# Third position of odd steps: one VectorE add out of PSUM in place of a ScalarE copy and a GpSimd add

## The chip, the cores and the metric

The kernel runs on one core of a Trainium2 chip. The metric is the device time of one execution in microseconds (us); lower is better. Engines are called as in the profile: PE (TensorE), PEld (TensorE's weight load), DVE (VectorE), ACT (ScalarE), POOL (GpSimd) and SP (SyncE). A "q" behind a name (ACTq, SPq) is the engine's sequencer, which also issues DMAs.

## What is computed

The input x is 32 images of 384 channels of 64x64, all fp32. Each image's channels are group-normalised in 32 groups of 12, displaced by a whole number of pixels (one displacement for every 8 channels, 48 of them), convolved channel by channel with a 5x5 Gaussian kernel that belongs to the displacement, and added to x:

```python
off_round = jnp.round(offset)
disp = _displace(x.reshape(B, P, cpp, h, w), off_int).reshape(B, C, h, w)
sub = offset - off_round
d = field[None] + sub[:, None, None, :]
kernel = jnp.exp(-jnp.sum(d * d, axis=-1) / (2.0 * SIGMA ** 2))
kernel = kernel / jnp.sum(kernel, axis=(1, 2), keepdims=True)
out = lax.conv_general_dilated(disp, kw, ..., feature_group_count=C)

x = x + _L0_conv_ref(_gn(x), L0_conv_offset)
```

Displacement and Gaussian are separable, so each is one matrix along y and one along x, and the whole is two chains of matmuls.

## The kernel before

**Tiling.** The channels are cut into 16 superblocks of 24 channels (3 displacements, called positions, of 8 channels). For a superblock the 32 images go through in 16 steps of 2 images. A step's tile `xin[:, s]` has 128 partitions and 6 x 256 fp32 (1536 elements); there are 16 such slots, so a slot is reused one superblock later. There are 256 steps, in 128 pairs of an even and an odd step.

**A pair on PE** (`two_steps`), in program order: the y products of positions 1 and 2 of the even step (position 0 was done at the end of the pair before, in `begin_even`), with the sums of the statistics between them (`sum_stats`, line 632); the y products of the odd step (all line 640); `x_products(0)` and `x_products(1)` (line 651) of the even and of the odd step. PE's results lie in `ps`, PSUM, as `ps[:, v]` for the even (v = 0) and the odd step (v = 1), four banks each. The x products of positions 0 and 1 go to banks 0 and 1 of their half, those of position 2, the "third position", to banks 2 and 3. `x_done` counts twice in a step: after positions 0 and 1, and after position 2.

**The other engines.** All follow a program order written out by hand, and talk by semaphores.

- ACT: copies y out of PSUM (`copy_y`, line 563; for the odd step three lanes of four), issues the stores of the step two behind, normalises half of a later step (line 552), and copies the third position from PSUM to the buffer `x2` (`copy_third`, line 581). At a superblock's last step it also fills the y matrices of the next one (`fill_rows`, line 541), in three parts with the two copies between them.
- DVE: in each pair the last lane's y copy (`copy_last_lane`, line 462), `add_x` for the even and the odd step (line 469: PSUM of positions 0 and 1, 1024 elements, plus `xin`, into `xin`), six `bn_stats` of 512 elements (line 441) for the pair four ahead, and between the fifth and the sixth the reduction of the summed statistics (`sums`, line 451). Once in a superblock, at step 11, also `values` (line 428).
- POOL: for each of the two steps the other half of the normalisation (line 301); once in a pair the seven small instructions of the coefficients (lines 276 to 287, `rstd` line 285 the longest) and the two of the summands (lines 259 and 261), for which PE's `sum_stats` waits; then `add_third` for the even and the odd step (line 292: `x2` plus `xin` into `xin`, 512 elements). Behind `add_third` of step 3 comes `whole_distances` (`t_int`, line 234), behind that of step 5 `full_distances` (`t_full`, line 240), behind that of step 15 `column_matrices` (`ax`, line 248).
- SP: loads the slots, each as soon as its last store has landed.

**What ties them.** `result0_ready` counts third positions that are added, `result1_ready` the rest; a store waits for both. `x2_ready` counts copies into `x2` and starts at 1. Before PE overwrites `ps[:, 1]` (first y product of an odd step) and `ps[:, 0]` (`begin_even`) it waits for `x2_ready` and `result1_ready`.

Of the kernel before, what the change touches and what calls it, by code (L numbers as in the profile page):

```python
# [6 lines left out]
ALU = mybir.AluOpType  # L7
ACT = mybir.ActivationFunctionType
# [3 lines left out]
P = 128  # L12
# [9 lines left out]
QP = Q // POS  # L22
GROUPS = 2
QG = Q // GROUPS
ROW = R * HW
# [7 lines left out]
PAIR = 2  # L33
# [12 lines left out]
def displaced_conv(nc: bass.Bass, x: bass.AP, offset: bass.AP, out: bass.AP):  # L46
# [7 lines left out]
    with ExitStack() as ctx:  # L54
        def sb(name, shape, dt=F32):
            return ctx.enter_context(nc.sbuf_tensor(name, shape, dt))

        def sem(name):
            return ctx.enter_context(nc.semaphore(name))


        xin = sb("xin", [P, SLOTS, Q, ROW])
        norm = sb("norm", [P, 2, R, Q * HW])

        y = sb("y", [P, 2, POS, R, LANES, 32])
        x2 = sb("x2", [P, 2, QP, ROW])

        stats = sb("stats", [P, RING, PAIR, CHUNKS, 3 * GROUPS])
        summands = sb("summands", [P, PAIR, CHUNKS, 3 * GROUPS])
# [57 lines left out]
        ps = ctx.enter_context(nc.psum_tensor("ps", [P, 2, LANES, 512], F32))  # L127
# [22 lines left out]
        x_done = sem("x_done")  # L150
        x2_ready = sem("x2_ready")
        result0_ready = sem("result0_ready")
        result1_ready = sem("result1_ready")
# [16 lines left out]
        ADDS = 2  # L170
# [38 lines left out]
        def _(pool):  # L209
# [19 lines left out]
            def whole_distances(c):  # L229
                if c is 0:  # L230
                    pool.wait_ge(shifts, 1)
                else:
                    pool.wait_ge(made, c)
                pool.tensor_tensor(t_int[:], grid[:, None, :, :].to_broadcast([P, POS, KINDS, HW]),  # L234
                                   place[:, bass.ds(POS * c, POS), :].unsqueeze(3).to_broadcast([P, POS, KINDS, HW]),
                                   ALU.add).then_inc(dist_ready, 1)
# [52 lines left out]
            def add_third(t, s):  # L289
                pool.wait_ge(x2_ready, t + 1 + SPARE)  # L290
                at = xin[:, s, 4:6, :]
                pool.tensor_tensor(at, x2[:, s % 2], at, ALU.add).then_inc(result0_ready, 1)  # L292

            def normalise(t, s, pair, first=False):
                pool.wait_ge(coef_ready, pair + 1)
# [21 lines left out]
            def step(c, s, head, tail):  # L317
                t, p = STEPS * c + s, STEPS // PAIR * c + s // PAIR
                if not (tail and s + PAIR >= STEPS):
                    normalise(t + PAIR, (s + PAIR) % STEPS, STEPS // PAIR * c + (s + PAIR) // PAIR)  # L320
                if s % PAIR == 1:
                    if not (tail and s // PAIR + LEAD >= STEPS // PAIR):
                        coefficients(p + LEAD, (s // PAIR + LEAD) % 2)
                    if not (tail and s // PAIR + LEAD + 1 >= STEPS // PAIR):
                        make_summands(p + LEAD + 1, (s // PAIR + LEAD + 1) % RING)
                    else:

                        pool.engine_nop().then_inc(summands_ready, PAIR)
                    add_third(t - 1, s - 1)
                    add_third(t, s)  # L330
                if not tail:
                    if s == 3:
                        whole_distances(c + 1)
                    if s == 5:
                        full_distances(c + 1)
                    if s == STEPS - 1:
                        column_matrices(c + 1)
            run(step)

        @block.vector  # L340
        def _(dve):
# [124 lines left out]
            def add_x(t, s):  # L466
                dve.wait_ge(x_done, ADDS * t + 1)
                at = xin[:, s, 0:4, :].rearrange("p (k h) f -> p h k f", h=QP)
                nc.vector.tensor_tensor(at, ps[:, s % 2, 0:2].rearrange("p h (k f) -> p h k f", k=2), at,  # L469
                                        ALU.add).then_inc(result1_ready, 1)  # L470

            def all_statistics(s):
                for part in range(CHUNKS):
# [47 lines left out]
        def _(act):  # L521
# [55 lines left out]
            def copy_third(t, s, first=False):  # L577
                act.wait_ge(x_done, ADDS * (t + 1))
                if not first:
                    act.wait_ge(result0_ready, t - 1)  # L580
                nc.scalar.activation(x2[:, s % 2], ps[:, s % 2, 2:4, 0:ROW], ACT.Copy).then_inc(x2_ready, 1)  # L581

            def store(c, s, t):
                act.wait_ge(result0_ready, t + 1)
# [4 lines left out]
            def step(c, s, head, tail):  # L589
                t = STEPS * c + s  # L590
                copy_y(t, s % 2, head and s <= 1)
                if s >= BEHIND:
                    store(c, s - BEHIND, t - BEHIND)
                elif not head:
                    store(c - 1, s - BEHIND + STEPS, t - BEHIND)
                border = s == STEPS - 1 and not tail
                if border:
                    fill_rows(c + 1, 0)
                if s % PAIR == 1:
                    copy_third(t - 1, s - 1, head and s == 1)  # L600
                if border:
                    fill_rows(c + 1, 1)
                    copy_third(t, s)
                    fill_rows(c + 1, 2)
                if not (tail and s + PAIR >= STEPS):
                    normalise(t + PAIR, (s + PAIR) % STEPS, STEPS // PAIR * c + (s + PAIR) // PAIR, False)
                if s % PAIR == 1 and not border:
                    copy_third(t, s, head and s == 1)
                if not tail:
                    if s == 5:  # L610
                        square(c + 1, 0)
                    if s == 7:
                        square(c + 1, 1)
                    if s == 9:
                        exponential(c + 1)
            run(step)

            act.wait_ge(norm0_ready, TOTAL)
# [7 lines left out]
        def _(pe):  # L626
# [35 lines left out]
            def two_steps(one):  # L662

                two, three = pe.snap(one + 1), pe.snap(one + 2)
                pe.wait_ge(norm1_ready, one)
                pe.wait_ge(mats_ready[1], one)
                y_product(1, 0)
                pe.wait_ge(summands_ready, one)
                sum_stats(0)
                pe.wait_ge(mats_ready[2], one)  # L670
                y_product(2, 0)

                pe.wait_ge(x2_ready, one)
                pe.wait_ge(result1_ready, one)
                pe.wait_ge(norm0_ready, two)
                y_product(0, 1)
                pe.wait_ge(norm1_ready, two)
                y_product(1, 1)
                y_product(2, 1)
                pe.wait_ge(ax_ready, one)  # L680
                pe.wait_ge(sums_ready, one)
                pe.wait_ge(y_ready, one)
                pe.sem_inc(x_started, 1)
                x_products(0)
                pe.wait_ge(last_lane_ready, one)
                pe.wait_ge(y_ready, two)
                pe.sem_inc(x_started, 1)
                x_products(1)

                pe.wait_ge(x2_ready, two)  # L690
                pe.wait_ge(result1_ready, two)
                begin_even(three)
# [31 lines left out]
```

## Time and profile before

| what | value |
|---|---|
| median of 3 runs | 1200.35 us (1197.65 to 1202.0) |
| the profiled execution | 1203.69 us, of which the span from the first to the last instruction is 1201.8 us |
| granted TensorE clock, mean | 0.996 |
| busy share of the span: PE, POOL, DVE, ACT | 96%, 81%, 76%, 66% |
| DMA | 335 GB/s over the span, each queue about half of the 16 engines' time |

The time outside the span is 1.9 us. In the views, a row of a group has: line, engine, operation, output and inputs with their shapes, count, then busy us and mean ns of one, then the idle time of the engine just before them and what ended it. A row of the timeline has: start and length in us from the span's start, engine, line, operation; in square brackets the idle time before it and what ended that.

### The profile page before, as it was taken

The page shows a single profiled execution, that of the slowest core. Times are in us where ns is not written, and L with a number is a line of the kernel's source. Part 1 is how long each engine was busy: PE and PEld are TensorE (multiplying, and loading weights), DVE is VectorE, ACT ScalarE, POOL GpSimd, SP SyncE. Part 2 cuts the span into 40 slices and gives each one's busy share as a digit, 9 for nine tenths or more (in the row PEclk, how much of TensorE's full clock was granted, in tenths as well). Part 3 has the DMA queues.
Part 4 walks back from the last instruction along what each step waited for, and adds up shares of the span by engine and source line. Part 5 has one row for each costly group of instructions (what it writes and reads, how often), then busy time and mean ns, then how long its engine had stood idle before and what let it go on. Part 6 is the DMA issues. An engine that isn't in the chain of part 4 may idle for free.

```text
span 1201.8 us, 113371 instructions
## 1 busy us (share of the span) xinstructions
PE 1159.0 (96%) x50224; PEld 1129.6 (94%) x50224; DVE 913.3 (76%) x1338; ACT 792.8 (66%) x915; POOL 970.4 (81%) x1734
## 2 busy tenths in 40 slices
PE   1899999999999999999999999999999999999997
PEld 1899999999999999999999999999999999999997
DVE  7578777777877777877777877777777777877773
ACT  3477667676666676666676666666666766666654
POOL 5488878878887888878878888887888888788874
PEclk9899999999999999999999999999999999999999
DMA  6899999999999999999999999999999999999966
GB/s 211 283 337 350 347 351 349 348 353 345 351 341 348 349 344 351 344 352 346 352 344 344 353 343 347 352 345 351 341 352 347 346 350 350 343 347 345 344 205 209
DMA packets 409760, 402.92 MB, mean 335 GB/s; under 512 B 16529, under 2 KB 409745, under 8 KB 409745
## 3 DMA queue, kind: packets, MB, share of 16 engines
q1 hardware_dynamic: 204944, 201.41, 51.6%
q10 hardware_dynamic: 204800, 201.36, 48.9%
q14 instruction: 13, 0.10, 0.0%
q8 instruction: 3, 0.05, 0.0%
HBM read 201.38 MB, written 201.33 MB: 335 GB/s over the span
## 4 chain that ended last, share of the span: by engine, by line
PE 89%; POOL 3%; issue 2%; ACTq 2%; ACT 1%; POOLq 0%; DVE 0%; DVEq 0%
PE ps L640 58%; PE ps L651 29%; PE ps L632 2%; ACTq L587 2%; POOL t_full L240 1%; ACT ay L541 1%; ACT x L581 1%; POOL norm L301 0%; POOL rstd L285 0%; POOL xin L292 0%; POOL summands L259 0%; POOL summands L261 0%; DVE stats L441 0%; POOLq L54 0%; POOL spread L281 0%
## 5 line engine op out<-in xcount | busy, mean ns | idle before, releaser
L640 PE MATMUL ps<-ay,norm 32*128 32x128 f32 x24608 | 762.0, 276 | 11.8 <-ACT x L581 6.3
L640 PEld LDWEIGHTS ps<-ay,norm 32*128 32x128 f32 x24608 | 723.0, 188 | 21.6 <-issue 13.4
L563 ACT ACTIVATE y<-ps 128x1536 f32<-128x1536 f32 (+1 forms) x256 | 330.2, 1290 | 257.2 <-PE ps L640 257.1
L441 DVE BATCH_NORM_STATS2 stats<-xin 128x6 f32<-128x512 f32 x768 | 487.4, 691 | 0.0
L651 PE MATMUL ps<-ax,y 64*64 64x64 f32 x24576 | 408.9, 220 | 4.4 <-issue 4.4
L651 PEld LDWEIGHTS ps<-ax,y 64*64 64x64 f32 x24576 | 389.4, 135 | 21.7 <-issue 4.6
L469 DVE TENSOR_TENSOR xin<-ps,xin 128x1024 f32<-128x1024 f32 x256 | 313.4, 1224 | 98.4 <-PE ps L651 98.1
L301 POOL TENSOR_SCALAR norm<-xin,rstd,bias 128x768 f32<-128x768 f32 x256 | 260.5, 1020 | 127.3 <-PE ps L640 107.4
L292 POOL TENSOR_TENSOR xin<-x,xin 128x512 f32<-128x512 f32 x256 | 320.3, 1272 | 11.2 <-ACT x L581 10.9
L552 ACT ACTIVATE norm<-xin,bias,rstd 128x768 f32<-128x768 f32 x256 | 261.7, 1022 | 34.9 <-issue 34.3
L581 ACT ACTIVATE x<-ps 128x512 f32<-128x512 f32 x256 | 151.0, 590 | 85.9 <-PE ps L651 85.7
L451 DVE TENSOR_REDUCE both<-ps 128x12 f32<-128x144 f32 x128 | 39.4, 308 | 136.8 <-ACT y L563 134.4
L285 POOL TENSOR_TENSOR rstd<-var,mhalf 128x4 f32<-128x4 f32 x128 | 130.2, 1017 | 10.0
L462 DVE COPY y<-ps 128x384 f32<-128x384 f32 x128 | 71.3, 557 | 41.5 <-PE ps L640 41.5
L632 PE MATMUL ps<-summands,ones 32*128 32x36 f32 x1040 | 47.9, 246 | 20.6 <-POOL summands L261 20.5
L632 PEld LDWEIGHTS ps<-summands,ones 32*128 32x128 f32 x1040 | 44.5, 190 | 22.8 <-issue 16.1
L541 ACT ACTIVATE ay<-t_msk,same 128x256 f32<-128x256 f32 x96 | 44.7, 523 | 12.3 <-issue 10.4
L261 POOL TENSOR_TENSOR summands<-stats 128x12 f32<-128x12 f32 x128 | 27.2, 213 | 19.5 <-POOL summands L259 19.3
L281 POOL TENSOR_TENSOR spread<-inner,both 128x4 f32<-128x4 f32 x128 | 26.0, 203 | 10.7
L234 POOL TENSOR_TENSOR t_int<-grid,place 128x960 f32<-128x960 f32 x16 | 28.8, 1800 | 7.0 <-DVEq L408 7.0
L283 POOL TENSOR_TENSOR var<-spread,mean_sq 128x4 f32<-128x4 f32 x128 | 26.4, 206 | 10.0
L278 POOL TENSOR_SCALAR inner<-both 128x4 f32<-128x4 f32 x128 | 25.4, 199 | 10.8
(54 smaller groups left out, 223.3 us busy)
## 6 DMA issues: line engine op xcount, KB each, us to landing
xin<-in_x_dram SPq DMA_DIRECT2D x512, 384.0 KB, 6.8
out_dram<-xin ACTq DMA_DIRECT2D x512, 384.0 KB, 6.8
off<-in_L_conv_offset_dram SPq DMA_DIRECT2D x1, 48.0 KB, 3.6
```

What stands on the lines that cost most here:

```text
L285: pool.tensor_tensor(rstd[:, v], var[:, v], mhalf[:, :], ALU.pow).then_inc(small, 1)
L292: pool.tensor_tensor(at, x2[:, s % 2], at, ALU.add).then_inc(result0_ready, 1)
L301: pool.tensor_scalar(norm[:, s % 2, :, cols].rearrange("p r (q w) -> p q r w", w=HW), xin[:, s, QG:].rearrange("p q (r w) -> p q r w", w=H ...
L441: nc.vector.bn_stats(stats[:, s // PAIR % RING, s % PAIR, n, :], xin[:, s].rearrange("p (g q) f -> p q f g", g=GROUPS)[:, n]).then_inc(bn_ ...
L462: nc.vector.tensor_copy(y[:, 1].rearrange("p k r a m -> p a (k r) m")[:, LANES - 1], ps[:, 1, LANES - 1, 0:POS * P].rearrange("p (n m) -> ...
L469: nc.vector.tensor_tensor(at, ps[:, s % 2, 0:2].rearrange("p h (k f) -> p h k f", k=2), at, ALU.add).then_inc(result1_ready, 1)
L552: nc.scalar.activation(norm[:, s % 2, :, cols].rearrange("p r (q w) -> p q r w", w=HW), xin[:, s, 0:QG].rearrange("p q (r w) -> p q r w", ...
L563: nc.scalar.activation(y[:, v].rearrange("p k r a m -> p a (k r) m")[:, 0:lanes], ps[:, v, 0:lanes, 0:POS * P].rearrange("p a (n m) -> p a ...
L581: nc.scalar.activation(x2[:, s % 2], ps[:, s % 2, 2:4, 0:ROW], ACT.Copy).then_inc(x2_ready, 1)
L632: last = nc.tensor.matmul(ps[:, v, a, SUMS], ones[rows, :], summands[rows].rearrange("p t n s -> p (t n s)"), start=True, stop=True)
L640: last = nc.tensor.matmul(ps[:, v, a, P * k:P * (k + 1)], norm[rows, v, r, P * k:P * (k + 1)], ay[rows, k, r, :], start=(r == 0), stop=(r ...
L651: last = nc.tensor.matmul(ps[outs, v, 2 * (k // 2) + h, at:at + HW], y[rows, v, k, r].rearrange("p a m -> p (a m)")[:, outs], ax[rows, k], ...
```

## The change

The third position of odd steps no longer goes by ACT's copy to `x2` and POOL's add. DVE adds it itself: in `add_x` of an odd step it waits for the second count of `x_done` and adds `ps[:, 1, 2:4, 0:256]` (512 elements a partition) to `xin[:, s, 4:6]`, and only then counts `result1_ready`. `x2` becomes a single buffer, ACT and POOL count for two steps at once (`then_inc(..., PAIR)`), and PE's wait for `x2_ready` in the middle of the pair goes away, since `result1_ready` covers it.

```diff
-        x2 = sb("x2", [P, 2, QP, ROW])
+        x2 = sb("x2", [P, QP, ROW])
...
             def add_third(t, s):
                 pool.wait_ge(x2_ready, t + 1 + SPARE)
                 at = xin[:, s, 4:6, :]
-                pool.tensor_tensor(at, x2[:, s % 2], at, ALU.add).then_inc(result0_ready, 1)
+                pool.tensor_tensor(at, x2[:], at, ALU.add).then_inc(result0_ready, PAIR)
...
                     add_third(t - 1, s - 1)
-                    add_third(t, s)
...
             def add_x(t, s):
                 dve.wait_ge(x_done, ADDS * t + 1)
                 at = xin[:, s, 0:4, :].rearrange("p (k h) f -> p h k f", h=QP)
-                nc.vector.tensor_tensor(at, ps[:, s % 2, 0:2].rearrange("p h (k f) -> p h k f", k=2), at,
-                                        ALU.add).then_inc(result1_ready, 1)
+                added = nc.vector.tensor_tensor(at, ps[:, s % 2, 0:2].rearrange("p h (k f) -> p h k f", k=2), at,
+                                                ALU.add)
+                if s % PAIR == 1:
+
+                    dve.wait_ge(x_done, ADDS * (t + 1))
+                    at = xin[:, s, 4:6, :]
+                    added = nc.vector.tensor_tensor(at, ps[:, 1, 2:4, 0:ROW], at, ALU.add)
+                added.then_inc(result1_ready, 1)
...
-                nc.scalar.activation(x2[:, s % 2], ps[:, s % 2, 2:4, 0:ROW], ACT.Copy).then_inc(x2_ready, 1)
+                nc.scalar.activation(x2[:], ps[:, 0, 2:4, 0:ROW], ACT.Copy).then_inc(x2_ready, PAIR)
...
                 if border:
                     fill_rows(c + 1, 1)
-                    copy_third(t, s)
                     fill_rows(c + 1, 2)
...
-                if s % PAIR == 1 and not border:
-                    copy_third(t, s, head and s == 1)
...
-                pe.wait_ge(x2_ready, one)
                 pe.wait_ge(result1_ready, one)
                 pe.wait_ge(norm0_ready, two)
                 y_product(0, 1)
```

On POOL the place is the end of the pair of steps 4 and 5, where `t_full` stands behind the adds. Before:

```order
81 L261 TENSOR_TENSOR summands<-stats 128x12
82 L292 TENSOR_TENSOR xin<-x,xin 128x512 x2
83 L240 TENSOR_TENSOR t_full<-t_int,sub 128x960
84 L301 TENSOR_SCALAR norm<-xin,rstd,bias 128x3x4x64 x2
85 L276 TENSOR_TENSOR mean_sq<-both 128x4
```

The same place of the changed kernel:

```order
81 L261 TENSOR_TENSOR summands<-stats 128x12
82 L292 TENSOR_TENSOR xin<-x,xin 128x512
83 L240 TENSOR_TENSOR t_full<-t_int,sub 128x960
84 L301 TENSOR_SCALAR norm<-xin,rstd,bias 128x3x4x64 x2
85 L276 TENSOR_TENSOR mean_sq<-both 128x4
```

One add of 512 elements is left ahead of `t_full`, and everything behind it moves up by one instruction.

On DVE the place is any pair, here the first of the program, from the reduction on. Before:

```order
55 L451 TENSOR_REDUCE both<-ps 128x12 [waits stat_summed,y_ready,coef_ready]
56 L441 BN_STATS stats<-xin 128x6
57 L462 COPY y<-ps 128x12x32 [waits y_done]
58 L469 TENSOR_TENSOR xin<-ps,xin 128x2x2x256 [waits x_done] x2
59 L441 BN_STATS stats<-xin 128x6 [waits first_summands,loaded8]
60 L441 BN_STATS stats<-xin 128x6 x2
```

The same place of the changed kernel:

```order
55 L450 TENSOR_REDUCE both<-ps 128x12 [waits stat_summed,y_ready,coef_ready]
56 L440 BN_STATS stats<-xin 128x6
57 L461 COPY y<-ps 128x12x32 [waits y_done]
58 L468 TENSOR_TENSOR xin<-ps,xin 128x2x2x256 [waits x_done] x2
59 L474 TENSOR_TENSOR xin<-ps,xin 128x512 [waits x_done]
60 L440 BN_STATS stats<-xin 128x6 [waits first_summands,loaded8]
```

A third add stands between the odd step's add and the six `bn_stats`, with a wait of its own. PE's own instructions stay as they are.

## Rows read from the trace of the kernel before

**Rows 1.** The page: busy us, share of the span, instructions.

```profile
PE 1159.0 (96%) x50224; PEld 1129.6 (94%) x50224; DVE 913.3 (76%) x1338; ACT 792.8 (66%) x915; POOL 970.4 (81%) x1734
```

**Rows 2.** Timeline of PE alone, from step 2's x products on, and the last pair.

```profile
196.69 3.35 PE L651 MATMUL ps<-ax,y 64*64 64x64 f32 x192
199.98 2.09 PE L640 MATMUL ps<-ay,norm 32*128 32x128 f32 x64
...
205.79 3.03 PE L651 MATMUL ps<-ax,y 64*64 64x64 f32 x192
208.75 2.08 PE L640 MATMUL ps<-ay,norm 32*128 32x128 f32 x64
210.64 0.34 PE L632 MATMUL ps<-summands,ones 32*128 32x36 f32 x8
...
214.56 3.03 PE L651 MATMUL ps<-ax,y 64*64 64x64 f32 x192
217.53 2.07 PE L640 MATMUL ps<-ay,norm 32*128 32x128 f32 x64
219.82 0.43 PE L632 MATMUL ps<-summands,ones 32*128 32x36 f32 x8 [0.22 <-POOL summands L261]
...
1191.31 3.03 PE L651 MATMUL ps<-ax,y 64*64 64x64 f32 x192
```

**Rows 3.** Waits of PE and of its weight loads: us in total, times, longest.

```profile
PE ps L640 <- ACT x L581: 6.3, 16, 0.7
...
PEld ps L632 <- POOL summands L261: 6.5, 10, 3.3
```

**Rows 4.** Timeline, POOL, steps 5 to 7.

```profile
210.40 2.49 POOL L292 TENSOR_TENSOR xin<-x,xin 128x512 f32<-128x512 f32 x2
...
212.86 1.79 POOL L240 TENSOR_TENSOR t_full<-t_int,sub 128x960 f32<-128x960 f32 x1
...
214.65 1.95 POOL L301 TENSOR_SCALAR norm<-xin,rstd,bias 128x768 f32<-128x768 f32 x2
...
217.86 1.02 POOL L285 TENSOR_TENSOR rstd<-var,mhalf 128x4 f32<-128x4 f32 x1
...
219.56 0.21 POOL L261 TENSOR_TENSOR summands<-stats 128x12 f32<-128x12 f32 x1 [0.15 <-POOL summands L259]
```

**Rows 5.** Timeline, POOL, an odd step's normalisation that waits for PE.

```profile
197.00 0.98 POOL L301 TENSOR_SCALAR norm<-xin,rstd,bias 128x768 f32<-128x768 f32 x1 [1.21 <-PE ps L640]
```

**Rows 6.** Groups by form: the adds of POOL and of DVE.

```profile
L292 POOL TENSOR_TENSOR xin<-x,xin 128x512 f32<-128x512 f32 x256 | 320.3, 1272 | 11.2 <-ACT x L581 10.9
L469 DVE TENSOR_TENSOR xin<-ps,xin 128x1024 f32<-128x1024 f32 x256 | 313.4, 1224 | 98.4 <-PE ps L651 98.1 <-issue 0.2
```

**Rows 7.** Timeline, DVE, an ordinary pair.

```profile
213.56 0.31 DVE L451 TENSOR_REDUCE both<-ps 128x12 f32<-128x144 f32 x1 [0.89 <-ACT y L563]
...
214.76 0.56 DVE L462 COPY y<-ps 128x384 f32<-128x384 f32 x1 [0.27 <-PE ps L640]
...
217.19 1.23 DVE L469 TENSOR_TENSOR xin<-ps,xin 128x1024 f32<-128x1024 f32 x1 [0.18 <-PE ps L651]
```

**Rows 8.** Timeline, a pair in which DVE also runs `values`.

```profile
168.27 0.31 DVE L451 TENSOR_REDUCE both<-ps 128x12 f32<-128x144 f32 x1 [0.97 <-ACT y L563]
...
170.16 0.56 DVE L462 COPY y<-ps 128x384 f32<-128x384 f32 x1
```

**Rows 9.** One line's view of `rstd` (ns min/median/max).

```profile
L285 POOL TENSOR_TENSOR rstd<-var,mhalf x128: 1007/1017/1029, 19.4 to 1176.3; 128x4 f32<-128x4 f32 x128
```

**Rows 10.** Timeline, PE's first y products behind a superblock's border.

```profile
616.05 2.07 PE L640 MATMUL ps<-ay,norm 32*128 32x128 f32 x64 [0.27 <-ACT x L581]
```

**Rows 11.** Timeline, the end of the program.

```profile
1193.68 2.66 POOL L292 TENSOR_TENSOR xin<-x,xin 128x512 f32<-128x512 f32 x2 [6.10 <-ACT x L581]
1193.94 1.23 DVE L469 TENSOR_TENSOR xin<-ps,xin 128x1024 f32<-128x1024 f32 x1 [0.17 <-PE ps L651]
...
1194.98 3.15 ACTq L587 DMA_DIRECT2D out_dram<-xin  x4
```

## The prediction

> **What bounds the kernel now.** The page's busy shares come first: PE is busy for 96% of the span, no other engine over 81% [rows 1]. So time is won or lost only where PE's stream is longer than it need be, and the next view is the timeline of PE alone. The pair that begins with the x products at 205.79 ends where the next x products begin, at 214.56, that is after 8.77 us. The reader is to see its parts: 2.96 us of x products (205.79 to 208.75), 1.89 us until the sums of the statistics (208.75 to 210.64), and 3.92 us from there to the next x products [rows 2]. I take 8.77 us as PE's floor for a pair. From 205.79 to the last pair's x products at 1191.31 there are 109 pairs, so 9.04 us a pair [rows 2]: 0.27 us over the floor, about 34 us over the 126 full-speed pairs of the run.
>
> Where that excess lies decides the worth of the change. Three places:
>
> 1. *The sums wait for the summands, in the pair of steps 6 and 7.* There the y products begin at 217.53 and the sums at 219.82, after 2.29 us and not 1.89: PE stands for 0.40 us [rows 2]. The view of waits says who is late: PE's weight loads waited for POOL's summands 10 times, 6.5 us in all, 3.3 of them once [rows 3], and that one is the start of the program. So 9 of 16 superblocks lose 0.36 us, together 3.2 us.
> 2. *The superblock's border.* PE waits there for ACT's copy of the even step's third position, 6.3 us in 16 waits [rows 3], for instance 0.27 us at 616.05 [rows 10].
> 3. *Slower streams.* The rest, some 24 us, is in no wait: the same 192 x products take 3.29 us from 196.69 to 199.98 and 2.96 us from 205.79 to 208.75 [rows 2]. What slows them the views of before do not tell. Neither of the odd step's third-position instructions can overlap them, since both come after the odd step's x products.
>
> **Part by part.**
>
> *POOL loses one add a pair*, 1.272 us of mean length [rows 6], 163 us of work. POOL is not PE's bound in an ordinary pair: its odd normalisation waits for PE there (1.21 us in the pair at 196.69, where it starts 0.31 us after the x products [rows 2, 5]), and coefficients and summands follow it. An earlier end of the adds changes nothing for them, since the waiting normalisation stands in between. Only where a third long instruction is in that queue does the backlog reach the summands. At step 5 it does: the two adds start at 210.40, `t_full` at 212.86, the two normalisations run back to back from 214.65 to 216.60, and the summands end at 219.77, 0.05 us before PE's sums [rows 2, 4]. Without the second add (1.23 us of the 2.49) `t_full` runs from 211.63 to 213.42, the even normalisation to 214.40, and the odd one is again released by PE, at 214.56 + 0.31 = 214.87, so that it ends at 215.85 and not 216.60. All behind it moves up by 0.75 us, the summands to 219.02. PE would want them at 217.53 + 1.89 = 219.42. The 0.40 us are gone, with 0.4 to spare. *Term: -3.2 us.* If the seven visits too short for the view of waits have a little each, it is nearer 4.
>
> *ACT loses one copy a pair.* In ordinary pairs it comes last, ahead of a wait for PE. At the border, two of the three fills of the y matrices lie behind the even copy, for which PE waits, and nothing is taken from ahead of it. *Term: 0; the 6.3 us stay.*
>
> *PE loses one wait*, for the copy of the odd step a pair back, long done. *Term: 0.*
>
> *DVE gains one add a pair.* The trace has none of this shape. From below: half of the same add at 1024 elements, 0.61 us [rows 6]. From above: that whole add, 1.22, or what POOL takes for the same elements, 1.27 [rows 6]. Two rows of DVE reading PSUM give a line between: 384 elements in 0.56 us [rows 7], 1024 in 1.224 [rows 6], so 1.04 ns an element and, for 512, 0.69 us. I take that. The Trainium skill ("VectorE: DVE Perf Modes", the section on the TRN2 errata) charges VectorE 120 cycles ahead of a PSUM source and 58 ahead of an SBUF one, which speaks against moving work there; by it the add would be 0.66 us, an estimate, and the sum would not change. The wait for `x_done` costs nothing: the second count comes with the last x products (208.75 in one pair), and the first odd add ends later.
>
> Who pays for the 0.69 us? Behind the new add stand five `bn_stats`, then the reduction, the sixth `bn_stats`, the last-lane copy. The `bn_stats` work four pairs ahead and nobody waits for them. The reduction stood idle 0.89 us for ACT's y copy in an ordinary pair and 0.97 us in the pair with `values` [rows 7, 8]. It absorbs the add with about 0.2 us left, and the last-lane copy, which has another 0.27 us of idle time in an ordinary pair, starts as before. PE itself waits for the odd adds only before the next odd step's first y product. In the pair at 214.56 the old add ends at 218.42 [rows 7], the new one at 219.11, and that product comes behind the sums (219.82) and one y product of the even step. *Term: 0.* If the cover is gone it costs, above all in the pair with `values`: there the copy ends at 170.72, 1.45 us after the x products began, about where the odd step's half of them begins. At the upper bound of 1.27 the reduction would be 0.3 us late, 16 times: +5 us. The term lies between 0 and +5.
>
> *The end.* POOL's two last adds end at 1196.34, and DVE's last odd add would end at 1195.86 [rows 11]. But ACT has four DMAs to issue from 1194.98 on, 3.15 us in a row, so the last pair of them is hardly earlier [rows 11]. *Term: 0 to -0.1.*
>
> **Sum.** 1203.69 us for the profiled execution (span 1201.8 plus 1.9) less 3.2 gives 1200.5. The profiled execution is 3.3 us above the median of the runs, so against 1200.35 the forecast is 1197.2, 0.27% less. I take differences under 0.3%, 3.6 us, as none that a measurement of this kernel can tell; the forecast lies just inside, and a little more than my sum (4 us in place of 3.2) lies outside.
>
> **Rivals.**
>
> - *Given back in the streams.* The 24 us of slow x products depend on something that is not constant from pair to pair, and the freed pair is followed by another 0.4 us sooner. If that one runs like 196.69 (+0.33 us) in each superblock, 16 times, +5.3 us stand against -3.2: 1202.5, no change that can be told. For it: fast and slow streams stand two pairs from each other, so their state is short-lived [rows 2]. Against it: nothing links it to POOL. If two pairs more of eight go that way it is +10.6 - 3.2, 1207.7, slower. The same cause can go the other way: one pair in eight less slow gives 1192.
> - *DVE becomes the late one*, the case on the other side. The place is the last-lane copy in the pair with `values`. It decides from a price of about 0.97 us for the new add with its wait; at 1.27 it is +5, net +1.6, 1202. To be slower by over 3.6 us it would have to take 1.4 us, over every row, or be joined by the first rival.
> - *DVE's new add holds POOL up.* It runs (218.42 to 219.11 in that pair) just where POOL works on bias and summands. In an ordinary pair these are ready at 210.45 for sums at 210.64, so about 0.14 us after the hand-over are free; a POOL that stood for the whole 0.69 us would cost PE 0.55 us a pair, +66 us, 1263. Against it: an add of the same kind ran from 217.19 to 218.42 [rows 7] beside `rstd` at 217.86, which took 1.02 us [rows 4], and the longest of all 128 took 1.029 [rows 9]. The Trainium skill ("SBUF — State Buffer", Who interferes with whom) has a DVE instruction contend with GpSimd when both its inputs lie in SBUF; the new add has one in PSUM, so by that rule it does not, and the trace agrees.
> - *More is freed than I see.* If POOL and ACT, with less to do, also shorten the border (half of 6.3), it is 1194.
>
> **How the numbers follow.** The forecast as worked out, the stall gone and all else within 2 us: 0.50, at 1197.2, of which nearly half is beyond 0.3%. Given back in part or whole: 0.23, 1198 to 1203. More freed, or streams faster: 0.15, 1189 to 1194. DVE late: 0.06. Two pairs in eight slower: 0.05. POOL held up: 0.01. Faster by over 0.3%: 0.40; within: 0.46; slower: 0.14. The range leaves out the ends of these: 1190 to 1204.
>
> **What would show it.** PE's sums in the pair of steps 6 and 7 start 1.89 us after the y products in every superblock, and the waits for POOL's summands have only those of the start left. POOL busy falls by about 160 us to near 810, ACT by 75, DVE rises by about 85 to near 1000. The new add reads 0.69 us. The reduction's idle time falls from 0.9 to about 0.2 us and nothing behind it is late. The waits at the border stay near 6 us. The prediction is wrong if PE shows a wait for DVE's last-lane copy, if `rstd` or the summands get longer, or if the mean of the x products' streams moves.

## The result, and the profile after

The changed kernel took 1203.94 us in the median of 20 runs (1201.01 to 1207.43), the kernel before 1200.89 us (1197.45 to 1203.6, 20 runs). The ratio is 1.0031, with a 95% interval from 1.0023 to 1.0039: slower by about 3.7 us, where a time shorter by 3.2 us was forecast.

The page of the changed kernel begins with the busy shares, which answer to [rows 1]:

```profile
PE 1163.0 (97%) x50224; PEld 1135.4 (94%) x50224; DVE 990.0 (82%) x1466; ACT 737.4 (61%) x787; POOL 813.9 (68%) x1606
```

Its groups by line follow, with those of the x products, of POOL's adds, of the reduction and of the new add:

```profile
L653 PE MATMUL ps<-ax,y 64*64 64x64 f32 x24576 | 417.9, 221 | 3.4 <-issue 3.4
...
L292 POOL TENSOR_TENSOR xin<-x,xin 128x512 f32<-128x512 f32 x128 | 162.6, 1270 | 8.7 <-ACT x L586 8.7
...
L450 DVE TENSOR_REDUCE both<-ps 128x12 f32<-128x144 f32 x128 | 39.4, 308 | 58.5 <-ACT y L568 56.0
L474 DVE TENSOR_TENSOR xin<-ps,xin 128x512 f32<-128x512 f32 x128 | 87.1, 681 | 0.0
```

And the waits of PE and its weight loads, which answer to [rows 3]:

```profile
PE ps L642 <- ACT x L586: 6.4, 16, 0.6
...
PEld ps L634 <- POOL summands L261: 3.5, 2, 3.3
```

Nearly all that was said of the engines is there. The new add takes 0.681 us. POOL is busy for 156 us less and DVE for 77 more. ACT is busy for 55 us less, not 75: the group of its copies fell by 75 (151.0 to 76.0 us), but in the records a copy overlaps its neighbours by about 0.1 us on either side, and what overlaps counts once in the share. The reduction still waits for ACT, 56 us in place of 134, so nothing behind it is late. PE's waits for the summands are gone but for the start of the program. The border is the same. And PE is busy for 4 us longer: its x products take 417.9 us in place of 408.9, with the same 24576 instructions, while its y products and sums take 1.9 and 1.4 us less. These are the x products and the reduction in the kernel before:

```profile
L651 PE MATMUL ps<-ax,y 64*64 64x64 f32 x24576 | 408.9, 220 | 4.4 <-issue 4.4
...
L451 DVE TENSOR_REDUCE both<-ps 128x12 f32<-128x144 f32 x128 | 39.4, 308 | 136.8 <-ACT y L563 134.4 <-PE ps L632 2.4
```

PE's timeline of the changed kernel, from step 6's x products on, shows both sides. The columns are start and length:

```profile
222.12 3.28 PE L653 MATMUL ps<-ax,y 64*64 64x64 f32 x192
225.33 2.09 PE L642 MATMUL ps<-ay,norm 32*128 32x128 f32 x64
227.22 0.34 PE L634 MATMUL ps<-summands,ones 32*128 32x36 f32 x8
...
231.14 3.37 PE L653 MATMUL ps<-ax,y 64*64 64x64 f32 x192
234.44 2.09 PE L642 MATMUL ps<-ay,norm 32*128 32x128 f32 x64
```

The sums start 1.89 us after the y products (225.33 to 227.22), but the x products before them take 3.21 us, and in the next pair 3.30, where the floor is 2.96 [rows 2].

For all pairs but the first I took the same distances from the records of the trace. Two sums of them are used from here on. The **stream excess** is the time from the 97th to the last record of a pair's 192 x products (the odd step's half) over 1.36 us, which is what the fastest pairs need; the first 96 of the 192 take the same time in both kernels. The **summands' stall** is the time from the y products' start behind the x products to the next x products, over 5.82 us; the only wait of PE in that stretch is the one for the summands.

| kernel | stream excess | summands' stall | border and other waits ahead of the y products |
|---|---|---|---|
| before | 17.7 us | 4.4 us | 8.0 us |
| changed | 26.7 us | -0.1 us | 7.4 us |

The sum of the differences is +9.0 - 4.5 - 0.6 = +3.9 us, at 4.0 before rounding. From the second pair's x products to the last's the trace of the kernel before shows 1138.75 us and that of the changed one 1142.76, so these three hold the whole difference. (The start of the program, up to the second pair's x products, is 2.4 us shorter in this trace; it lies between 48.2 and 52.6 us in the 13 traces of this case.)

### The profile page after: what moved, and what is told of

The parts are those of the page before. It is cut to its first block, busy times and chain, and to the rows that moved or that the text cites. A ratio compares the mean times of both kernels' runs of the same rounds, so it can differ in the third digit from the quotient of the medians.

```text
span 1203.6 us, 113103 instructions
## 1 busy us (share of the span) xinstructions
PE 1163.0 (97%) x50224; PEld 1135.4 (94%) x50224; DVE 990.0 (82%) x1466; ACT 737.4 (61%) x787; POOL 813.9 (68%) x1606
## 4 chain that ended last, share of the span: by engine, by line
PE 92%; ACTq 2%; issue 2%; ACT 1%; DVE 0%; DVEq 0%
PE ps L642 60%; PE ps L653 30%; ACTq L592 2%; PE ps L634 2%; ACT x L586 1%; ACT ay L546 0%; DVE xin L468 0%; ACTq L182 0%; DVEq L54 0%; ACT y L568 0%; ACTq L585 0%; ACTq L544 0%; ACTq L567 0%; ACTq L554 0%
## 5 line engine op out<-in xcount | busy, mean ns | idle before, releaser
L653 PE MATMUL ps<-ax,y 64*64 64x64 f32 x24576 | 417.9, 221 | 3.4 <-issue 3.4
L653 PEld LDWEIGHTS ps<-ax,y 64*64 64x64 f32 x24576 | 398.1, 135 | 20.9 <-issue 3.5
L292 POOL TENSOR_TENSOR xin<-x,xin 128x512 f32<-128x512 f32 x128 | 162.6, 1270 | 8.7 <-ACT x L586 8.7
L586 ACT ACTIVATE x<-ps 128x512 f32<-128x512 f32 x128 | 76.0, 594 | 82.4 <-PE ps L653 81.2
L474 DVE TENSOR_TENSOR xin<-ps,xin 128x512 f32<-128x512 f32 x128 | 87.1, 681 | 0.0
```

The costliest lines, as they stand in the source:

```text
L292: pool.tensor_tensor(at, x2[:], at, ALU.add).then_inc(result0_ready, PAIR)
L474: added = nc.vector.tensor_tensor(at, ps[:, 1, 2:4, 0:ROW], at, ALU.add)
L586: nc.scalar.activation(x2[:], ps[:, 0, 2:4, 0:ROW], ACT.Copy).then_inc(x2_ready, PAIR)
L653: last = nc.tensor.matmul(ps[outs, v, 2 * (k // 2) + h, at:at + HW], y[rows, v, k, r].rearrange("p a m -> p (a m)")[:, outs], ax[rows, k], ...
```

## What is different where the streams are slow

In the second half of the x products the engines do the same work at the same moments in both kernels: the even step's add on DVE, the even copy on ACT, and but for two pairs of eight the coefficients on POOL. (The even copy starts 0.1 to 0.3 us later in the changed kernel, but it waits for x products of this very half.) Nor is it the clock: two windows of the kernel before, a slow and a fast run of x products, have 1.00 of it granted (the third column from the end):

```profile
196.69:199.98 3.29, 3.29 (x197) 3.22 (x193) 2.15 (x3) 2.66 (x4) 2.66 (x7) 1.00 1.07 367
205.79:208.75 2.96, 2.96 (x197) 2.89 (x193) 2.11 (x3) 2.35 (x4) 2.63 (x8) 1.00 1.06 357
```

Two things differ. The first is in ACT's program ahead of the odd step's y copy. `REGISTER_ALU` is an instruction of the sequencer that computes the value which a wait compares with. Before:

```
125 L560 REGISTER_ALU
126 L563 ACTIVATE y<-ps 128x3x12x32 [waits x_done,y_done]
127 L587 ISA [waits result1_ready,result0_ready]
128 L587 DMA out_dram<-xin 64x6x256
```

The changed kernel:

```
114 L565 REGISTER_ALU
115 L567 REGISTER_ALU [waits y_done]
116 L568 ACTIVATE y<-ps 128x3x12x32 [waits x_done]
117 L592 ISA [waits result1_ready,result0_ready]
```

The removed odd copy waited for `x_done` to reach 2(t+1), the very value that the next odd y copy waits for. The register with it was reused. With the copy gone the value has to be computed anew, behind the wait for `y_done`, where it delays the y copy and the store behind it. The timelines of ACT and of the loads show by how much. Before, with x products from 214.56 on:

```profile
214.69 1.13 ACT L563 ACTIVATE y<-ps 128x1152 f32<-128x1152 f32 x1
214.88 1.66 ACTq L587 DMA_DIRECT2D out_dram<-xin  x2
...
215.23 1.79 SPq L194 DMA_DIRECT2D xin<-in_x_dram  x2
```

After, with x products from 231.14 on:

```profile
231.35 1.13 ACT L568 ACTIVATE y<-ps 128x1152 f32<-128x1152 f32 x1
231.56 1.52 ACTq L592 DMA_DIRECT2D out_dram<-xin  x2
...
231.48 1.39 SPq L194 DMA_DIRECT2D xin<-in_x_dram  x2
```

The y copy starts 0.21 us into the x products and not 0.13, the store is issued at 0.42 and not 0.32. The second thing is the load: here it goes out 0.34 us in, just ahead of the store, while in the fast pair of the kernel before it came at 0.67, behind it. Counted over all pairs, odd steps' loads that go out 0.2 to 0.5 us into the x products are 82 of 126 after and 51 before. Pairs with such a load have a stream excess of 0.26 us after and 0.24 before, the others 0.12 and 0.07. I call these 0.2 to 0.5 us the slow phase of the loads. Three theories follow. Theory A: the register instruction, by moving the store, makes more pairs fall into the slow phase. Theory B: it is the missing stall that lets them drift there. Theory C: the new add on DVE does it by its traffic.

## Experiments

All ratios are to the kernel before, with 95% intervals. The stream excess and the summands' stall are those of one execution of each kernel, the profiled one. There is no E7 in the table: it was E11 with its two waits on SP in the other order, and it has no time.

| run | median us | ratio | stream excess | summands' stall |
|---|---|---|---|---|
| E1 before, store 0.15 us later | 1203.73 | 1.0026 (1.0015 to 1.0038) | 16.2 us | 5.7 us |
| E2 changed, register value given back | 1196.54 | 0.9973 (0.9960 to 0.9986) | 16.0 us | 0.2 us |
| E3 changed, odd loads behind the x products | 1191.67 | 0.9929 (0.9914 to 0.9944) | 5.1 us | 0.7 us |
| E4 before, the same delay | 1197.56 | 0.9982 (0.9970 to 0.9994) | 1.8 us | 11.2 us |
| E5 E2 and E3 together | 1191.43 | 0.9921 (0.9906 to 0.9935) | 2.6 us | 0.1 us |
| E6 changed, POOL's load as before | 1203.10 | 1.0022 (1.0011 to 1.0032) | 25.1 us | 0.0 us |
| E8 E2, odd loads held to the middle | 1186.90 | 0.9882 (0.9866 to 0.9898) | 3.0 us | 0.7 us |
| E9 before, loads held to the middle | 1195.85 | 0.9958 (0.9941 to 0.9974) | 1.6 us | 13.2 us |
| E10 changed, loads held to the middle | 1191.54 | 0.9922 (0.9906 to 0.9939) | 5.1 us | 1.0 us |
| E11 E2, loads forced to the slow phase | 1203.19 | 1.0020 (1.0003 to 1.0038) | 22.3 us | 0.3 us |
| E12 changed, nearly no loads | 1186.46 | 0.9884 (0.9865 to 0.9903) | 5.2 us | 2.2 us |

**E2, the register value alone.** The wait of the removed copy stays in its place on ACT, where nothing follows but a wait for PE:

```diff
                     normalise(t + PAIR, ...)
+                if s % PAIR == 1 and not border:
+                    act.wait_ge(x_done, ADDS * (t + 1))
```

> The changed kernel with the wait of the removed odd copy left in its place on ScalarE (the wait alone), which gives the odd step's y copy its register value again; the order of ScalarE's instructions ahead of the odd store is then that of before, and the store is issued 0.31 us after the x products begin. Theory A: the excess of the odd x products falls back to 17 to 20 us, the stall at steps 6 and 7 stays away, and the time is 1195 to 1198 (0.996 to 0.998), the forecast. Theory B and theory C: still 1203 to 1205, excess near 27.

It came as theory A said. The y copy and the store are back at 0.13 and 0.32 us into x products that begin at 219.84:

```profile
219.97 1.13 ACT L568 ACTIVATE y<-ps 128x1152 f32<-128x1152 f32 x1
220.16 1.48 ACTq L592 DMA_DIRECT2D out_dram<-xin  x2
```

and the x products need 10.5 us less than in the changed kernel:

```profile
L655 PE MATMUL ps<-ax,y 64*64 64x64 f32 x24576 | 407.4, 220 | 3.0 <-issue 3.0
```

At 0.9973 the kernel is where the forecast put the change (1197.2). DVE's add and the missing stall are both in it, with an excess of 16.0 us, so theories B and C are out as the cause of the slow streams. The edit gives back the wait and, with it, the value; the two were not tried apart. That it is the value is read from the programs and from the y copy, which starts 0.13 us into the x products with it and 0.21 without.

**E1, the same lateness put into the kernel before.**

```diff
                 if not first:
+                    if v == 1:
+                        act.wait_ge(x_done, ADDS * (t - 1) - 1)
                     act.wait_ge(x_done, ADDS * (t - 1))
```

> The kernel before with one redundant wait more ahead of the odd step's y copy on ScalarE, so that its sequencer issues the odd step's store about 0.1 us later, as in the changed kernel (0.42 us and not 0.31 us after the x products begin). Theory A (the changed kernel lost a cached register on ScalarE, its store is issued behind SyncE's load and not ahead of it, and the pairs lock into the phase in which the odd x products run slowly): the excess of the odd x products rises from 17.7 us to about 25 us, with POOL, DVE and PE's waits as before, and the time to about 1206 (1.005). Theory B (it is the missing 0.4 us stall at steps 6 and 7 that lets the pairs drift into the slow phase): no change beyond 0.2%, 1200 to 1203, excess near 18. Theory C (the new VectorE add slows PE or the DMAs): as B.

The total was slower, between theory A's 1206 and the 1200 to 1203 of the others, and not by the route that theory A gave. The extra wait cost more than 0.1 us: the store goes out 0.47 us in and not 0.32, the y copy ends at 1.39 us in place of 1.26, and the odd step's half of the x products begins 0.04 us late in each pair, 4 us in all. The summands' stall is 1.3 us larger. The streams' excess did not rise (16.2 us). So lateness of the store does not by itself bring the slow phase: only 64 of 126 loads went out at 0.2 to 0.5 us, with an excess of 0.15 us. This part of theory A fell; what E1 shows is that the y copy has no slack of 0.13 us.

The traces hold one thing more: what goes with a slow stream is less the load's moment than its distance from the store. In E1 the loads that go out 0.25 to 0.35 us in have an excess of 0.12 us, where those of the same moments have 0.27 in the kernel before and 0.25 in the changed one. One such pair of E1, with x products of 3.15 us from 211.89, a load at 0.32 and a store at 0.47:

```profile
211.89 3.21 PE L653 MATMUL ps<-ax,y 64*64 64x64 f32 x192
...
212.36 1.46 ACTq L589 DMA_DIRECT2D out_dram<-xin  x2
...
212.21 1.39 SPq L194 DMA_DIRECT2D xin<-in_x_dram  x2
```

Sorted by whether the odd load goes out within 0.15 us of the odd store, before or behind it, the pairs are these:

| kernel | store, us into the x products | pairs with a load that near | their excess | excess of the others |
|---|---|---|---|---|
| E1 | 0.47 | 43 | 0.18 us | 0.11 us |
| before | 0.32 | 47 | 0.25 us | 0.08 us |
| E2 | 0.32 | 55 | 0.21 us | 0.07 us |
| E11 | 0.32 | 71 | 0.24 us | 0.10 us |
| E6 | 0.42 | 75 | 0.26 us | 0.13 us |
| changed | 0.42 | 77 | 0.26 us | 0.15 us |

The distance was chosen with the traces at hand, and no run set it by itself.

**E6, POOL's load.** An add of 512 elements on constants into a spare buffer stands behind the even step's add, its result unused.

```diff
                     add_third(t - 1, s - 1)
+                    pool.wait_ge(spare_done, p + 1)
+                    pool.tensor_tensor(spare..., twice, twice, ALU.add).then_inc(spare_done, 1)
```

> The changed kernel in which GpSimd runs, behind the even step's add, an add of the same 512 elements on constants into a spare buffer (its result goes nowhere), so that its load is that of before. Theory B (the stall at steps 6 and 7 keeps the pairs out of the slow phase): the stall is back, about 3 us, but the excess of the odd x products falls to 18, and the time to 1199 to 1201. Theory A: the stall is back and the excess stays near 25, so 1205 to 1208.

The streams stay slow, as theory A has it, but the stall did not come back, the time is no longer than the changed kernel's, and theory B is not tested by this run: the dummy takes 1.04 us and not 1.27, and where the x products take 0.25 us longer, PE comes to the sums that much later. The slow streams hide POOL's lateness. The kernel before has it too: the stall of 0.40 us at 219.82 follows x products of 2.97 us [rows 2].

**E3 and E4, the loads moved out of the way.** SP holds the load of an odd step's slot until the x products of the pair in which it would go out are done:

```diff
                     sync.wait_ge(stored[s], 16 * B * c)
+                    if s % PAIR == 1:
+                        sync.wait_ge(x_done, ADDS * (STEPS * (c - 1) + s + 5))
                     load(c, s)
```

> The changed kernel, in which SyncE issues an odd step's load not when its slot's store has landed (about 0.3 us into the x products) but when the x products of that pair are done, about 3 us in. Theory A and theory B share that the slow odd x products come with loads issued 0.2 to 0.4 us into the x products: both then expect the excess to fall below 10 us and the time to about 1185 (0.987). If the slow stream has nothing to do with the moment of the loads (theory C): no change, 1204.

> The kernel before with the same delay of the odd steps' loads. If the phase of the loads sets the speed of the odd x products in both kernels: about 1190, and 3 to 4 us slower than the changed kernel with the same delay, which is the stall at steps 6 and 7 alone. If not: 1201.

The excess falls in both, below 10 us as expected, though the totals fell less: the waits ahead of the y products, for ACT's even copy, grew to 14.9 us in E3 and 13.6 in E4, and in E4 the summands' stall grew to 11.2 us. The views of waits have these two:

```profile
PE ps L644 <- ACT x L588: 10.4, 23, 0.7
...
PE ps L642 <- ACT x L583: 10.3, 18, 0.8
```

At the border PE waits 9.6 us in E3 and 10.4 in E4, where it was 7.2 in the changed kernel and 6.7 before. The x products end 0.2 us sooner there than with slow streams, but the copy, with a fill of the y matrices ahead of it, ends 3.4 to 3.5 us after they begin in all four. So fast streams lose some 3 us of their gain at the border. In E3 most of the rest is in two other pairs, where the issues of the odd stores end 0.1 us later than in the changed kernel, and the even copy with them. E3 is 6.7 us above the 1185 expected, E4 7.6 us above its 1190. Between the two, the stall makes -10.5 us, the streams +3.3 and the waits ahead of the y products +1.3: E3 is 5.9 us faster, by the medians too.

**E5, both edits.**

> The changed kernel with both edits: the wait left in the place of the odd copy on ScalarE, and the odd steps' loads delayed until the x products of the pair are done. Theory A (the speed of the odd x products hangs on how loads and stores meet): with the loads out of the way the 0.1 us of ScalarE's issue no longer matters, so this is the same as the delay alone, 1190 to 1193, excess near 5 us. A theory in which ScalarE's extra register instruction costs time by itself expects a further 5 to 8 us, 1184 to 1187.

E5 and E3 cannot be told apart (1191.43 and 1191.67), as theory A had it; 1184 to 1187, for a register instruction that costs 5 to 8 us by itself, did not come.

**E9, E10 and E8, the odd loads held until the even step's x products are done** (`+ 4` in place of `+ 5`). They go out 1.83 us into the x products in every pair, as here in E8:

```profile
202.57 3.03 PE L657 MATMUL ps<-ax,y 64*64 64x64 f32 x192
...
204.40 1.91 SPq L194 DMA_DIRECT2D xin<-in_x_dram  x2
```

> The kernel before with the odd steps' loads held until the even step's x products are done, about 1.6 us into the x products. With the loads' moment fixed, the streams should run at the same speed in before and in the changed kernel, and what is left between them is what the change does on the engines: the wait for the summands at steps 6 and 7. Excess of the odd x products below 5 us; that wait 5 to 11 us in all, since PE comes to it sooner; 1193 to 1197.

> The changed kernel with the same hold of the loads and without the wait left on ScalarE. Theory A: with the store always ahead of the load, ScalarE's 0.1 us no longer matters: 1186 to 1188, as with that wait (1186.9). If the extra register instruction costs by itself, 1190 and more. Against the kernel before with the same hold it should be 6 to 9 us faster: the change's own worth.

> The same kernel with the load held until the even step's x products are done, about 1.6 us into the x products. Theory A in its narrow form: the store is always first, the load 1.2 us behind it, so the excess is small, below 8 us, and the time 1189 to 1193. If it is the running of a load's first packets beside the odd x products that slows them, whatever came first: excess 25 us or more, 1204.

With the loads' moment fixed, before and after differ by 4.3 us (1195.85 and 1191.54), less than the 6 to 9 expected, and the sign is that of the forecast. What is gained lies in the waits for the summands. In E9:

```profile
PEld ps L634 <- POOL summands L263: 13.1, 29, 3.3
```

where E10 has only those of the start:

```profile
PEld ps L636 <- POOL summands L263: 3.5, 2, 3.3
```

By the distances the stall makes -12.2 us here; +3.5 us of streams and +1.9 us of waits ahead of the y products stand against it. Of E9's 13.2 us of stall 8.0 lie behind the x products of steps 6 and 7 and 4.2 behind those of steps 4 and 5. E9's timeline shows the stall of steps 6 and 7 at fast streams:

```profile
211.09 3.03 PE L653 MATMUL ps<-ax,y 64*64 64x64 f32 x192
214.06 2.07 PE L642 MATMUL ps<-ay,norm 32*128 32x128 f32 x64
216.41 0.43 PE L634 MATMUL ps<-summands,ones 32*128 32x36 f32 x8 [0.28 <-POOL summands L263]
```

E8 is the fastest kernel here that loads its whole input, 1.2% under the kernel before and 2 us under its range. It is 4.6 us under E10, where theory A expected the same of both; E10's 1191.5 is what its rival said, a register instruction that costs by itself. In E10, E3 and E12 each pair has a stream excess of 0.04 to 0.05 us, together 5.1 or 5.2; in E5, E8, E4 and E9 it is 1.6 to 3.0. The first three share the y copy that starts 0.08 us later, and the store that goes out 0.10 us later. So this lateness costs 2 to 3.5 us by itself, whatever the loads do; whether by the copy or by the store these runs do not separate. (In E1 a still later copy delays the odd half's begin, which speaks for the copy.) The rest of the 4.6 us is not between the profiled executions (1188.57 and 1189.25), and between E3 and E5 the total shows no difference at all.

**E11, the slow phase forced on E2.** The same kind of hold, but for the odd step's y products, so that no odd load goes out earlier than some 0.2 us into the x products:

```diff
+                    if s % PAIR == 1:
+                        sync.wait_ge(y_done, STEPS * (c - 1) + s + 5)
                     sync.wait_ge(stored[s], 16 * B * c)
```

> The kernel with the wait left on ScalarE (1196.5), in which SyncE besides holds an odd step's load until the y products of that pair are done, so that it goes out 0.2 to 0.4 us into the x products wherever it would have come earlier. Theory A in its narrow form (a load issued just ahead of ScalarE's store makes the odd x products slow): excess 25 us or more, 1203 to 1206. If only the order of arrival in the pair before matters: 1196 to 1198.

The loads stand at 0.2 to 0.5 us in 87 of 126 pairs; those have an excess of 0.23 us, the rest 0.05. In the pair whose x products begin at 202.01 the load goes out 0.28 us in:

```profile
202.29 1.40 SPq L194 DMA_DIRECT2D xin<-in_x_dram  x2
```

and the x products take 3.27 us there, and 3.22 in the pair behind it:

```profile
202.01 3.33 PE L657 MATMUL ps<-ax,y 64*64 64x64 f32 x192
205.28 2.08 PE L646 MATMUL ps<-ay,norm 32*128 32x128 f32 x64
...
211.09 3.29 PE L657 MATMUL ps<-ax,y 64*64 64x64 f32 x192
214.31 2.08 PE L646 MATMUL ps<-ay,norm 32*128 32x128 f32 x64
```

The engines' programs are those of E2 but for SP's, the time is 6.7 us above E2's and the excess 6.3 us above it (22.3, where 25 or more was expected). That is the slow phase made by hand. The profiled execution is one of the fastest of E11's 12 (1199.96 of 1198.84 to 1206.89) and only 4.5 us above E2's: its waits ahead of the y products are 2.0 us less.

**E12, nearly no loads.** Behind the first superblock each load brings one of its 64 rows of partitions; the rest of the input is left out.

> The changed kernel, in which each load behind the first superblock brings one of its 64 rows of partitions only, so that nearly all load traffic is left out, and the results are those of stale data. Theory A: without loads no odd x products are slow, the excess is below 2 us, and the time is 1170 to 1180. If the stores alone can slow them: excess over 10 us.

The slow streams are gone, but for the 0.04 us a pair above (5.2 us, where less than 2 was expected): from 210.16 the x products take 3.00 us.

```profile
210.16 3.07 PE L654 MATMUL ps<-ax,y 64*64 64x64 f32 x192
213.16 2.13 PE L643 MATMUL ps<-ay,norm 32*128 32x128 f32 x64
```

The time, 1186.5, is above the 1170 to 1180 expected: the waits ahead of the y products, nearly all at the border (8.3 us), the pair with `values` (its x products' odd half begins 0.13 us late, 2.1 us in all) and the start do not hang on the loads. What is left of the loads goes out 1.9 us (even) and 4.9 us (odd steps) into the x products, so E12 takes away the traffic and the slow phase together. E8 reaches the same time with all its loads.

## Why the prediction was wrong

**What held.** The bound: PE, with no other engine in its way. The floor of 8.77 us a pair. The place and the size of the gain: the stall in the pair of steps 6 and 7, -3.2 us from the view of waits and "nearer 4" with the short visits; the distances give 4.5, of which 3.9 behind the x products of steps 6 and 7. The price of the new add: 0.69 us expected, 0.681 measured. Its cover: the reduction's idle time fell from 0.9 to 0.3 us in most pairs, and nobody waited for DVE longer than before. In the pair with `values` the x products' odd half begins 0.13 us late in both kernels, 2.2 us in all before and 2.1 after. The border, left as it was. That DVE would not hold up POOL: `rstd` still takes 1.017 us. One size was off without harm: of the "some 24 us" put down to slower streams 17.7 were, and the rest lay in the pair with `values` and in waits too short for the view.

**The step that failed** is "*ACT loses one copy a pair.* In ordinary pairs it comes last, ahead of a wait for PE. [...] *Term: 0; the 6.3 us stay.*" Of the instruction that was removed I counted the engine's time, and not what its wait left for the next one: a register value. Its absence put one sequencer instruction between PE's signal and the y copy. E2, which gives back that wait and its value and nothing else, is 7.4 us faster than the changed kernel by the medians and 7.0 by the ratios. The term should have been +7, with the sum near 1204.

**The way it costs** was a rival, "given back in the streams", at 0.23 and +5.3 us, which I held apart from the change ("nothing links it to POOL"). The streams took 9.0 us more and turned -4.5 into +3.9. The link was there, but by ACT and not by POOL: E2 shows that ACT's instruction brings most of it, and the traces point to ACT's store and SP's load. The last of the signs given for being wrong is the one that came: the mean of the x products' streams moved. Of the 9.0 us, 2 to 3.5 are the lateness of ACT by itself, as E3, E10 and E12 have it, and the rest goes with more loads 0.2 to 0.5 us into the x products (82 pairs and not 51), an attribution worked out from the traces. E11 shows that this phase costs 6 to 7 us where it is imposed, E8 and E12 that without it, or without loads, the excess is 3 to 5 us.

**What stays open.** Why the store's move lets more pairs settle there. E1, with a store that is later still, did not do it (64 pairs, excess 0.15 us); by the table at E1 its loads lie near the store in 43 pairs only, and what sets how often load and store meet was not tried. How the 7.4 us divide between ACT's lateness by itself (copy and store) and the phase: by the totals E8 against E10 says 4.6 for the lateness, E3 against E5 says 0.2, and the distances say 2 to 3.5. And what, physically, slows PE's matmuls beside a load in that phase.

## What to carry to other kernels

An instruction that is taken away takes its wait and its registers with it: look at the sequencer's instructions ahead of the next critical one, not only at the engine's. Where an engine is busy all the time, compare its busy time in the same group between two kernels before its waits; here PE's stall fell by 4.5 us and the group of the x products rose by 9. Where loads and stores keep the DMA engines busy all the time (the second column from the end in the two windows above, 1.07 and 1.06), the moment at which a load is issued is a thing to set, by a wait on the busy engine's progress, and not to leave to the landing of a store: that alone was worth 4.6 us to the kernel before (E9) and 12.4 to the changed one (E10), and 9.6 to E2 (E8).

## What the hardware showed that was not expected

The same 192 matmuls took 2.96 or 3.3 us with no wait on record, at a granted clock of 1.00 in both cases, and the difference followed the moment of a load's issue, or its distance from the store's. The Trainium skill ("SBUF — State Buffer", Who interferes with whom) says that DMA never contends with a compute engine and that PE never waits on anyone. Of a port conflict nothing here is shown, and no wait is on record. But the stream excess was 22.3 us in E11 and 16.0 in E2, 5.2 in E12 and 26.7 in the changed kernel, and only SP's loads differ within each of the two comparisons. So, taken as a statement on the time of PE's stream, the sentence does not hold for what these runs measure. The register instruction between the wait and the activation cost 0.08 us between a semaphore and the start of the activation (0.21 us in place of 0.13).
